# A selective scan rewritten from sequences to time steps

## What is computed

```python
proj = xs @ xproj_w
dt = softplus(proj[..., :D_INNER] + dt_bias)
Bm = proj[..., D_INNER:D_INNER + D_STATE]
Cm = proj[..., D_INNER + D_STATE:]
A = -exp(A_log)
def step(hst, ins):
    dt_t, B_t, C_t, x_t = ins
    dA = exp(dt_t[:, :, None] * A)
    hst = hst * dA + (dt_t * x_t)[:, :, None] * B_t[:, None, :]
    y_t = einsum('bds,bs->bd', hst, C_t)
    return (hst, y_t)
```

## Time and profile before

| | us |
|---|---|
| median of the runs | 7788.17 |
| span of the profiled execution | 7785.8 |
| conditioning, first loads | about 52 |
| preparation | 812 |
| scan (864.7 to 5432.4) | 4568 |
| finish_scan | about 265 |
| two transformer layers | about 2090 |

### The profile page before, as it was taken

The page is one execution under the profiler, slowest core; times in us unless marked ns, Lnnn a source line. Parts: engine busy times, 40 slices in busy tenths (PEclk is TensorE's granted clock), DMA queues, the critical chain, the costliest instruction groups (busy, mean ns, idle before and its releaser), DMA issues. The chain is left out here.

```text
span 7785.8 us, 230318 instructions
## 1 busy us (share of the span) xinstructions
PE 6767.1 (87%) x93480; PEld 3552.4 (46%) x93480; DVE 6075.5 (78%) x3804; ACT 5841.4 (75%) x8254; POOL 1947.6 (25%) x983
## 2 busy tenths in 40 slices
PE   6888688888888888888888888887989999978888
PEld 3434344444444444444444444444335455444444
DVE  2555799999999999999999999998435444345554
ACT  3555699999999999999999999997225344345554
POOL 1111122222222212221222222222003223133333
PEclk8999799999999999999999999999999999989999
DMA  6666522222222222222222222222620000000000
GB/s 191 149 153 156 120 70 66 69 69 69 66 69 69 67 69 69 69 66 68 69 69 67 67 70 69 66 69 74 225 97 6 9 9 9 3 32 12 12 12 6
DMA packets 621669, 540.95 MB, mean 69 GB/s; under 512 B 490880, under 2 KB 529408, under 8 KB 607040
## 3 DMA queue, kind: packets, MB, share of 16 engines
q1 hardware_dynamic: 614400, 524.52, 23.4%
q10 hardware_dynamic: 6208, 1.57, 0.1%
HBM read 380.46 MB, written 145.49 MB: 68 GB/s over the span
## 5 line engine op out<-in xcount | busy, mean ns | idle before, releaser
L1430 DVE TENSOR_TENSOR_SCAN s_h<-s_decay,s_h 128x2080 f32<-128x2080 f32 x1024 | 4540.3, 4510 | 6.4 <-ACT s_decay L1352 5.3
L1314 ACT COPY s_h<-s_pb 128x1024 f32<-128x1024 f32 x2044 | 2511.8, 1229 | 53.0 <-PE s_pb L1245 41.4
L1258 PE MATMUL s_py<-s_h,s_cz 128*32 128x128 f32 x32768 | 2512.3, 436 | 4.3 <-DVE s_h L1430 4.2
L1352 ACT ACTIVATE s_decay<-s_pa 128x1024 f32<-128x1024 f32 x2048 | 2168.1, 1059 | 89.6 <-DVE s_h L1430 57.1
L1385 POOL TENSOR_TENSOR s_cz<-s_cl,s_one 128x128 f32<-128x128 f32 x256 | 905.4, 3537 | 3347.9 <-PE s_py L1258 3335.9
L1258 PEld LDWEIGHTS s_py<-s_h,s_cz 128*32 128x32 f32 x32768 | 1032.0, 122 | 468.0 <-issue 4.5
L2207 ACT ACTIVATE t_prob<-t_ps,t_nmax 128x256 f32<-128x256 f32 x1024 | 479.5, 482 | 275.7 <-DVE t_nmax L2348 274.8
L1226 PE MATMUL s_pa<-az,s_al 18*128 18x64 bf16 x16384 | 424.6, 192 | 299.3 <-ACT s_decay L1352 247.9
L1226 PE MATMUL s_pa<-s_dl,s_al 18*128 18x64 bf16 x16384 | 423.6, 191 | 287.0 <-ACT s_decay L1352 274.4
L1969 POOL TENSOR_TENSOR t_prob<-t_prob,t_rinv 128x512 f32<-128x512 f32 x512 | 528.7, 1039 | 508.4 <-DVE t_rinv L2342 508.4
L1226 PEld LDWEIGHTS s_pa<-az,s_al 18*128 18x128 bf16 x16384 | 302.6, 94 | 470.0 <-ACT s_decay L1352 434.6
(11 more groups left out here) (254 smaller groups left out, 6341.6 us busy)
## 6 DMA issues: line engine op xcount, KB each, us to landing
s_al<-A SPq DMA_DIRECT2D x256, 144.0 KB
az<-B SPq DMA_DIRECT2D x512, 72.0 KB
az<-U SPq DMA_DIRECT2D x512, 72.0 KB
az<-D SPq DMA_DIRECT2D x512, 72.0 KB
s_bl<-B SPq DMA_DIRECT2D x512, 72.0 KB
s_ul<-U SPq DMA_DIRECT2D x512, 72.0 KB
s_dl<-D SPq DMA_DIRECT2D x512, 72.0 KB
D<-p_dp SPq DMA_DIRECT2D x64, 384.0 KB, 6.5
```

The costliest lines, as they stand in the source:

```text
L1258: mm = pe.matmul(py[e % 2][QR * q:QR * q + QR, 0:P], cz[e % 2][:, l * P + QR * q:l * P + QR * q + QR], states, start=(l == 0), stop=(l == ...
L1314: act.copy(out, pb[:].rearrange("p b t d -> p d b t")).then_inc(bu_done, count)
L1352: act.activation(decay[(z + e + at) % RING][:, part, 1:W], pa[j % 2][:], ACT.Exp).then_inc(exp_done, 1)
L1430: dve.tensor_tensor_scan(seg, decay[(z + e + j) % RING][:].rearrange("p d w -> p (d w)"), seg, 0.0, ALU.mult, ALU.add).then_inc(scanned, 1)
```

## The change

`scan` is written anew. The partitions stay (2 sequences) x (64 states); the columns are now the 8 units times 256 channels, 2048 columns, and one step is one time step of all of them. There are 4 sweeps (direction, half of the channels) of 256 steps, 1024 steps. The 2048 columns are four chunks of 512.

Chunks 0 and 1 stay in PSUM (`pA`): VectorE multiplies them in place by the decay (`times`), PE adds u B by accumulating onto what VectorE wrote (`to_a`), and ScalarE copies the result to SBUF for the y product (`copy_a`). For chunks 2 and 3, GpSimd multiplies the state of the step before by the decay, in SBUF (`decayed`), PE makes u B in `pB` (`to_b`), and VectorE adds the two into the next state (`plus`). The states `hs` have two buffers.

The decays of 8 steps are made ahead into one of two buffers `dec`: PE makes dt * A by channel, 64 columns being (8 steps, 8 units), read from `dl` with a stride of 64 elements (`adt`), and ScalarE takes the exp of 512 columns at a time, reading PSUM with a stride and writing runs of 8 channels (`take`). Two pairs of such exps stand in every step. y is gathered over 16 steps (a body) in one PSUM bank by sliding the window into `cz`, then transposed and stored.

In `prepare`, the projection for dt is made with tokens on the partitions (the same number of matmuls), its bias is a full tile `dtbb`, xs is transposed in place of u and VectorE multiplies it by dt (`take_u`), the cast of u is one operation of 2048 columns, and the first remainder goes to GpSimd (`first_rest_u`). C is stored with every second group of 8 steps reversed, by four copies in place of two. The parts are stored in the layouts of the new scan, and `load_first_tile` is gone. `finish_scan` reads y in the new layout.

```diff
+                def first_rest_u(i, r):
                     n = 2 * i + r
-                    wait(pool, s["dt_done"], n + 1)
-                    wait(pool, s["xs_done"], n + 1)
-                    wait(pool, s["ut_mm"], 4 * n)
...
+                def to_dt(i, r, tiles):
                     wait(pe, s["xs_done"], 2 * i + r + 1)
-                    for m in columns:
+                    for q in tiles:
                         for k in range(IC):
-                            mm = pe.matmul(g0[:, m, :], xp_w[r][:, k, m * P:(m + 1) * P], xs[r][:, k, :],
+                            mm = pe.matmul(g0[:, q, :], xs[r][:, k, q * P:(q + 1) * P], xp_w[r][:, k, 0:DI],
                                            start=(k == 0), stop=(k == IC - 1))
-                    if IC - 1 in columns:
...
-                        mm = pe.transpose(g1[:, q % 2, m * P:(m + 1) * P], u[:, m, q * P:(q + 1) * P], ident[:])
+                        mm = pe.transpose(g1[:, q % 2, m * P:(m + 1) * P], xs[r][:, m, q * P:(q + 1) * P], ident[:])
...
+                def take_u(i, r, some=range(4)):
                     n = 2 * i + r
+                    wait(dve, s["dt_done"], n + 1)
+                    wait(dve, s["up0"], n)
+                    wait(dve, s["ures"], n)
                     for q in some:
-                        wait(dve, s["up0"], 4 * n + q + 1)
-                        dve.tensor_tensor(ur[:, q, :], g1[:, q % 2, :], up[:, 0, q, :], ALU.subtract).then_inc(s["ures"], 1)
...
+    SWEEPS = 4
+    CH = 4
+    TB = 8
+    TU = 4
+    BODY = 16
+    BODIES = T // BODY
+    ALL = SWEEPS * BODIES
+    HALF = DI // 2
+    DS = P // 2
+    W = 2 * HALF
+    PAIRS = 16
+    BANKS = 3
+    CW = 304
...
+        dec = [sb(f"dec{e}", [P, TB, UNITS, HALF]) for e in range(2)]
+        hs = [sb(f"hs{k}", [P, 2, W]) for k in range(CH)]
+        cz = sb("cz", [P, UNITS, CW])
...
+        pA = c.enter_context(nc.psum_tensor("s_pA", [P, 2, W], F32))
+        pB = c.enter_context(nc.psum_tensor("s_pB", [P, 2, W], F32))
+        pa = c.enter_context(nc.psum_tensor("s_pa", [P, BANKS, W], F32))
+        py = c.enter_context(nc.psum_tensor("s_py", [P, W], F32))
...
+        def bodies(eng, body):
+            made = 2 * T - 2
+            body(0, 0, True, False, True, None)
+            with eng.Fori(0, SWEEPS - 1) as i:
+                for q in range(1, BODIES + 1):
+                    body(BODIES * i + q, made * i + 2 * (BODY * q - q // BODIES), q == BODIES, False, False,
+                         64 * i + 128 if q == BODIES - 1 else None)
+            for q in range(1, BODIES):
+                body(ALL - BODIES + q, made * (SWEEPS - 1) + 2 * BODY * q, False, q == BODIES - 1, False, None)
...
+                def adt(p, w, banks):
+                    wait(pe, taken, 2 * p - 1)
+                    for i in range(8):
+                        for e in range(2):
+                            q, d = 2 * (w[1] % 2) + e, 8 * (w[1] // 2) + i
+                            mm = pe.matmul(pa[:, banks[e], DS * i:DS * (i + 1)],
+                                           al[QR * q:QR * q + ROWS, d, :],
+                                           dl[w[0]][QR * q:QR * q + ROWS].rearrange("p t i d -> p (t i) d")[:, :, d],
+                                           start=True, stop=True)
+                    mm.then_inc(filled, 1)
+                def bu(out, k, x, first, signal):
+                    j, t = x // TU, x % TU
+                    r = slice(QR * k, QR * k + ROWS)
+                    for v in range(2):
+                        mm = pe.matmul(out[:, HALF * v:HALF * (v + 1)], bl[j % 2][r, t, v, :], ul[j % 2][r, t, v, :],
+                                       start=first, stop=True, skip_group_check=not first)
+                    mm.then_inc(signal, 1)
+                def to_a(n, x, k):
+                    wait(pe, mul, 2 * n + k + 1)
+                    bu(pA[:, k, :], k, x, False, bu_a)
+                def to_b(n, x, G, k):
+                    if k == 2 and x % TU == 0:
+                        uses = 2 * G + x // (2 * TU) + 1
+                        wait(pe, u_in[x // TU % 2], UQ * uses)
+                        wait(pe, b_in[x // TU % 2], BQ * uses)
+                    wait(pe, added, 2 * n - 3 + k)
+                    bu(pB[:, k - 2, :], k, x, True, bu_b)
+                def y(n, x, v):
+                    if v == 0:
+                        wait(pe, copied, 2 * n + 2)
+                        wait(pe, added, 2 * n + 2)
+                    at = 34 * x if x < 8 else 36 * (15 - x) + 2
+                    for k in range(CH):
+                        mm = pe.matmul(py[QR * k:QR * (k + 1), HALF * v:HALF * (v + 1)],
+                                       cz[:, 2 * k + v, at:at + QR], hs[k][:, x % 2, HALF * v:HALF * (v + 1)],
+                                       start=(x == 0 and v == 0), stop=(x == BODY - 1), skip_group_check=True)
                     mm.then_inc(y_mm, 1)
...
+                def produce(G, x, w, head, first_of):
+                    of = x // TB
+                    if x % TB == 0 and w == 0:
+                        wait(pe, d_in[1 - of], DQ * (G + 1 + of))
+                    if w == 0 and x % 2 == 0 and of and first_of is not None:
+                        wait(pe, a_in[x % TB // 2], first_of)
+                    adt(pair(G, x, w, head), (1 - of, 2 * (x % TB) + w),
+                        [slot_bank(0, w, x, head, e) for e in range(2)])
+                def body(G, made, first, last, head, turn):
+                    for x in range(BODY):
+                        n = BODY * G + x
+                        more = not (last and x >= TB)
+                        late = x == 1
+                        before = (x - 1) % BODY
+                        has = not (head and x == 0)
+                        to_a(n, x, 0)
+                        if more:
+                            produce(G, x, 0, head, turn)
+                        to_a(n, x, 1)
+                        if has and not late:
+                            if x == 2:
+                                wait(pe, c_filled, 2 * G + 1)
+                            if x == 9:
+                                wait(pe, c_filled, 2 * G + 2)
+                            y(n - 1, before, 0)
+                        if more:
+                            produce(G, x, 1, head, turn)
+                        if not (last and x == BODY - 1):
+                            to_b(n + 1, (x + 1) % BODY, G + (x + 1) // BODY, 2)
+                        if has and not late:
+                            y(n - 1, before, 1)
+                        if not (last and x == BODY - 1):
+                            to_b(n + 1, (x + 1) % BODY, G + (x + 1) // BODY, 3)
+                        if late:
+                            wait(pe, ytok_done, G)
+                            wait(pe, c_filled, 2 * G + 1)
+                            for v in range(2):
+                                y(n - 1, before, v)
+                        if x == 2 and not head:
+                            turn_y(15 + 33 * G + 6, G, [(12 + e) % BANKS for e in range(2)])
...
+                def take(p, at, i, bank, w):
+                    q, d = 2 * (at % 2) + i, 8 * (at // 2)
+                    act.activation(
+                        dec[w][:].rearrange("p t i d -> p (t i) d")[:, :, DS * q + d:DS * q + d + 8],
+                        pa[:, bank, :].rearrange("p (d c) -> p c d", d=8), ACT.Exp).then_inc(taken, 1)
+                def copy_a(n, x, k):
+                    wait(act, bu_a, 2 * n + k + 1)
+                    act.copy(hs[k][:, x % 2, :], pA[:, k, :]).then_inc(copied, 1)
+                def take_pair(G, x, w, head):
+                    p = pair(G, x, w, head)
+                    wait(act, filled, p + 1)
+                    for e in range(2):
+                        take(p, 2 * (x % TB) + w, e, slot_bank(0, w, x, head, e), 1 - x // TB)
+                def turned_y(p, G, banks):
+                    wait(act, filled, p + 1)
+                    wait(act, y_out, 32 * (G - 1))
+                    for v in range(2):
+                        for h in range(2):
+                            op = act.copy(ys[:, h].rearrange("p (k v) b t -> p v k b t", v=2)[:, v],
+                                          pa[:, banks[v], P * h:P * (h + 1)].rearrange(
+                                              "p (k t b) -> p k b t", k=CH, b=PAIR))
+                        op.then_inc(taken, 1)
+                def body(G, made, first, last, head, turn):
+                    for x in range(BODY):
+                        n = BODY * G + x
+                        more = not (last and x >= TB)
+                        copy_a(n, x, 0)
+                        if more:
+                            if x % TB == 0:
+                                wait(act, mul, 2 * n)
+                                wait(act, added, 2 * n)
+                            take_pair(G, x, 0, head)
+                        copy_a(n, x, 1)
```

(54 more changed lines are left out.)

652 lines of the change are left out of this document (251 added, 401 removed).

## The result

The kernel after takes 8567.65 us (median of four, 8565.26 to 8568.23) and the kernel before, run beside it, 7789.49 (7785.21 to 7791.39): 1.100 times as long, interval 1.0985 to 1.1016. I had forecast 6870. The profiled execution spans 8566.4 us, 780.6 more than before's 7785.8.

What follows compares the result with a forecast made beforehand. ScalarE was to bound the new scan at 3.28 us a step: 64 bodies of 56.5 us, 3616, plus start and end, 3646 against 4568 us, saving 922 of 7785.8, so 6870; range 6450 to 7650.

Steps and rivals of the forecast that it cites:

- TensorE's term: New scan, per step: u B 0.85, decay matmuls 0.66 and y 1.00 us, sum 2.5, behind ScalarE's 3.28.
- The clock: Scan's TensorE work priced at 2.4 GHz, granted 0.97 as in the kernel before: 107 ns per 256-column u B matmul.
- The stride: Scan's 32 decay matmuls, 2 x 0.33 us a step, if deltas 128 bytes apart are read as fast as packed ones.
- Rival 1: Strided deltas slow the scan's decay matmuls to 2.05 us a step, TensorE to 3.9; time 7420 or about 7740; chance 0.20.
- My counter-argument: Against a stride cost in the decay matmuls: today's u B matmuls read runs of 16 bytes at full speed; no size.
- rival 2: The scan's exps pay nothing for their stride: step 2.9 us, time 6475; chance 0.13.
- rival 3: In the scan VectorE and GpSimd exclude one another: 5.3 us a step, time 8660; chance 0.10.
- rival 4: Waits between five engines, ten handshakes a step, add 0.9 us to each scan step: time 7790; chance 0.07.
- Waits: ScalarE idles in each 16-step body: 1.2 us twice for decay buffers, 1.6 us for turning y.
- the start of the stage: Ahead of the scan's bodies: first loads 11 us and the first 16 pairs of exps 19 us.
- Preparation: Work moved between engines before the scan comes out even: 0 taken, with 38 us possible either way.
- ScalarE's step: Scan, per step: two copies at 0.48 and four exps at 0.58 us, 3.28 in all, setting the step.

Runs made afterwards that it cites:

- e5: Kernel after with deltas read packed and the u B matmuls reading all 128 rows instead of 18 (wrong sums): 6696.87 us.
- e10: Kernel after, deltas still strided, with only the u B matmuls widened to all 128 rows (wrong sums): 9406.36 us.
- e2: Kernel after with the decay matmuls reading 64 neighbouring deltas instead of every 64th (wrong output): 7816.47 us.
- e8: Kernel before with its y product over 32 rows instead of 128 in seven of eight matmuls (wrong sums): 8803.22 us.
- e11: Kernel after with packed deltas and six added 128-row bfloat16 matmuls of 256 columns in every step, u B at 18 rows: 9406.91 us.
- e7: Kernel after with packed deltas and the second half of y left out in 15 of 16 steps: 7153.51 us.
- e17: Kernel after, whole reference, with only TensorE's order changed: u B put between decay matmuls of other row groups; 7658.47 us, 0.984 of the kernel before.
- e13: Kernel after with packed deltas and u B over 64 rows (wrong sums): 8287.21 us.
- e1: Kernel after with 48 extra 128x128 float32 matmuls right before the scan's first step: 8575.23 us.
- e14 to e16: Kernel after with 48 matmuls before the scan, and: strided 128-row u B; whole reference, 128-row u B, earlier transfer; packed, six added matmuls. 9430.48, 9380.54, 9414.05 us.

## Why the prediction was wrong

**The step that failed is TensorE's term**, "Sum 2.5 us, so TensorE falls behind ScalarE". It was 4.93 us, and ScalarE waited for TensorE. Of the 2.42 us too few, 1.10 are in the decay matmuls, 1.02 in y and 0.30 in u B. Two things were wrong.

*The clock.* I priced u B at "107" ns a matmul "at the clock's 2.4 GHz; granted 0.97", and y at 1.00 us from a stage that runs at the high clock. y took twice that, and u B, though much of it ran beside other matmuls, 1.15 against 0.85, because the new scan's own mix of matmuls is granted 1.2 GHz. (Even at 1.00 y takes 1.15 in e5, in two halves.) That was an assumption without a row: the earlier trace rows gave the clock of a stage whose TensorE work the change replaces. What the clock costs with the stride in place is read within e10: 6.03 against 4.29 us a step, with u B over 128 rows. Packed, e5 is 1120 us below e2, although the wide form costs more where the clock is low (e10 against the kernel after, 839 us). That the height of the matmuls matters is shown from both sides: e5 (18 to 128 rows, clock 0.50 to 0.98) and e8 (128 to 32, 0.97 to 0.50), with unchanged instructions and columns. How rows, time and the rest combine is open: e11 added 128-row work and stayed low, e10 widened the same matmuls as e5 and was low most of the time. Nor do the runs separate the rows themselves from what comes with them, the overlap that is lost and the other values that are read. The Trainium skill (TensorE: Matmul & The Clock Gate, What's actually happening) says that the clock follows how busy the engine has been; the trace differs if busy means the records' time, which was 99% in the kernel after at 0.50 and 93% in e5 at 0.98.

*The stride.* "The 32 matmuls that fill the decays keep form and alternation, 2 x 0.33, if their deltas are read as fast as before": they were not, 2 x 0.88. Of the 1.10 us too few, 0.92 is the stride (2 x 0.42 packed at the same clock, e2). Rival 1 named this with a chance of 0.20 and its mechanism was right; its price with two row groups overlapping, 1.0 us a step, was too low against 1.76, and its other price, 2.05, a little high. I worked it out from a stream with four groups. The Trainium skill (Advanced Engine Details and Errata, Memory Cachelines) says that a new line for each access is penalised; the trace agrees, with 54 ns for 64 columns against 26 packed at 1.2 GHz. Whether 54 ns are one matmul after another or two that overlap at 108 is not shown. My counter-argument, that u B's runs of 16 bytes read at full speed, was about another case: by the same page such a run fills a line.

Rival 1 stopped short at 3.9 us, under 4.44, because it too took the high clock. The low clock without the stride (e2, 7816 us) makes the new scan about as long as the old one; the slowdown of 10% took both. The stride at the high clock alone, with u B over 18 rows, was never seen for a whole scan.

**What held.** *ScalarE:* exps 594 ns in duration (625 in e5), and 0.48 to 0.55 us each from start to start in e5 (two from 3000.65 to 3001.61 and from 3002.08 to 3003.19) where I had 0.58; the stride in PSUM costs nearly nothing, so rival 2 was the better reading: e5 steps in 3.02 us where nothing waits (copies at 3000.17 and 3003.19), between its 2.9 and my 3.28. *VectorE* 695 and 686 ns (0.69 taken, also where it writes PSUM), *GpSimd* 1274 (1264 taken): no exclusion, rival 3 is out although its 8660 us lies nearest to the result. *Handshakes:* e5 and e7 step at 3.02 and 3.43 us, so rival 4 is out. *Waits:* in e5 a body takes 53.9 us (891 steps in 3000 us by the count of copies) of which 16 x 3.02 is 48.3; 5.6 us of waits against my 4.0; the gap before an eighth step is 1.33 us for 1.2 (ScalarE's copy at 3007.56); the start of the stage was 43 us for 30. *Preparation:* as long in both, to 3 us. With the failed term taken away, as in e5, the kernel took 6697 us against 6870: the rest of the sum was 2.5% high. It is so near partly by luck, since ScalarE's step, 0.26 us too high, and the waits and the start, too low, offset each other in part.

**The range and the chances.** The high end, 7650, came from rival 1 at the high clock. The 0.14 for slower stood on rivals 3 and 4, whose mechanisms the trace doesn't show. No case had TensorE at 1.2 GHz, though the trace of before shows its scan at 0.50 for its first 40 us, with 18-row matmuls for decays and u B, the kinds that the change keeps.

## What to carry to other kernels

Price matmuls at the clock that the new mix of work will be granted, not at the one that the replaced stage had: look in the trace for a stretch in which only the kinds of matmul that remain are running. Read the moving operand's innermost stride before reusing a duration. And when matmuls use only part of the rows, order them so that neighbours use different row groups: e17, with not one instruction more or less in the loop, turned a kernel 10% slower than the one before into one 1.6% faster.

## What the runs showed of the hardware

- TensorE can have records 99% of the time and be granted 0.50 throughout (the kernel after, 1000 to 3000 us). With packed deltas the scan was granted 0.50 with u B over 18 rows (e2) or 64 (e13) and 0.98 with 128 (e5).
- A burst lifts the clock to 1.00 within some 10 us, and the steps bring it back to 0.50 about as fast (e1, e14 to e16).
- A kernel can run the same steps at both levels: e10's take 6.03 us at 0.50 and 4.29 at 1.00.
- The stride costs by time, not by clock: 16 decay matmuls 0.88 us at 0.50 and 0.87 at 1.00 (e1), 0.98 at both in e10. The strided y product of before is the same: 1.16 us at the low clock, 1.19 at the high one:

```profile
903.19 1.22 PE L1258 MATMUL s_py<-s_h,s_cz 128*32 128x128 f32 x16
904.35 0.39 PE L1245 MATMUL s_pb<-az 18*128 18x128 bf16 x4
```

- Matmuls in four row groups hide under one another (e17: 0.98 us for what took 0.88 and 0.5 and more apart). The Trainium skill (TensorE: Matmul & The Clock Gate, Part 3: Packing small matmuls — row/col tiling) says that matmuls of different row groups run concurrently; the trace agrees, also for strided operands.
- The 32-row form of y took 1.76 us where the 128-row form takes 1.16, at the same clock (e8). Not explained.
